# One block for the last three stages: both workspace stages and the adapter attention, with each stage's preparations placed inside the stage ahead of it

## The reference

```python
x = x + _L1_attn_a_ref(_layernorm(x, axis=-1), ...)   # gated linear attention
x = x + _L1_ffn_ref(_layernorm(x, axis=-1), ...)      # workspace stage
x = x + _L1_attn_b_ref(_layernorm(x, axis=-1), ...)   # adapter attention
x = x + _L1_ffn_ref(_layernorm(x, axis=-1), ...)      # workspace stage, same weights
```

```python
for _ in range(NB):                                   # NB = 2
    logits = _rms(x, norm_pre_w) @ compete_w.T + compete_b
    vals, idx = jax.lax.top_k(jnp.swapaxes(logits, 1, 2), k_eff)
    ...
    x_b = ctx @ out_proj_w.T + out_proj_b
    x = _rms(x + x_b, norm_post_w)
```

```python
base = jnp.einsum('bsd,od->bso', x, W)
low = jnp.einsum('bsd,brd->bsr', x, A[ids])
return base + jnp.einsum('bsr,bor->bso', low, B[ids])
```

## Time and profile before

| what | us |
|---|---|
| median of 3 executions | 2342.33 (2342.28 to 2348.39) |
| the profiled execution | 2342.52 |
| its span, first to last instruction | 2340.6 |
| workspace stage `wsa`, first product or statistic to last addition | 1705.5 to 1841.5 |
| adapter attention | 1846.1 to 2197.5 |
| workspace stage `wsb` | 2199.2 to 2333.1 |
| mean granted TensorE clock, 1 being full speed | 0.934 |

### The profile page before, as it was taken

The page is one execution under the profiler, slowest core; times in us unless marked ns, Lnnn a source line. Parts: engine busy times, 40 slices in busy tenths (PEclk is TensorE's granted clock), DMA queues, the critical chain, the costliest instruction groups (busy, mean ns, idle before and its releaser), DMA issues. The chain is left out here.

```text
span 2340.6 us, 29360 instructions
## 1 busy us (share of the span) xinstructions
PE 2006.8 (86%) x11208; PEld 1261.8 (54%) x11208; DVE 1037.4 (44%) x2255; ACT 798.4 (34%) x1757; POOL 514.9 (22%) x618
## 2 busy tenths in 40 slices
PE   7999999997499999999999998588677588889776
PEld 4556565665266766676676667222244244445443
DVE  4554545453323232333333222388644644435444
ACT  2544434352133223323332331233213234335232
POOL 2222323231111011111101000055411333342210
PEclk9999999998699999999999999689878889999788
DMA  6000000000000000000000000100000000000001
GB/s 248 1 1 1 1 1 1 1 1 31 0 1 1 1 1 1 1 1 1 1 1 1 1 1 1 65 0 1 0 1 1 1 1 1 1 1 2 1 1 37
DMA packets 9770, 23.98 MB, mean 10 GB/s; under 512 B 2448, under 2 KB 6304, under 8 KB 8864
## 3 DMA queue, kind: packets, MB, share of 16 engines
q1 hardware_dynamic: 8336, 18.92, 2.2%
q10 hardware_dynamic: 1296, 3.18, 0.4%
HBM read 20.00 MB, written 2.10 MB: 9 GB/s over the span
## 5 line engine op out<-in xcount | busy, mean ns | idle before, releaser
L1170 PEld LDWEIGHTS cos_ps<-cos_vx,cos_probs 128*128 128x128 f32 x2048 | 238.4, 191 | 33.6 <-issue 28.7
L1170 PE MATMUL cos_ps<-cos_vx,cos_probs 128*128 128x129 f32 x2048 | 239.5, 274 | 4.2 <-DVE cos_on L867 4.2
L1161 PE MATMUL cos_ps<-cos_qT,cos_kT 128*128 128x512 f32 x512 | 231.3, 596 | 1.4 <-ACT cos_qT L1023 1.4
L1052 ACT ACTIVATE cos_probs<-cos_ps 128x512 f32<-128x512 f32 x256 | 151.0, 598 | 161.9 <-PE cos_ps L1161 160.8
L366 ACT ACTIVATE probs<-sc,nmax 128x512 f32<-128x512 f32 (+3 forms) x256 | 132.6, 525 | 188.5 <-DVE nmax L229 186.4
L967 POOL TENSOR_TENSOR cos_qrs<-cos_qse,neg_half 128x4 f32<-128x4 f32 x64 | 64.5, 1008 | 511.2 <-DVE cos_qse L849 511.2
L473 PE MATMUL sc<-kT,qT 128*128 128x512 f32 (+3 forms) x512 | 171.6, 457 | 3.9 <-DVE probsT L241 2.5
L2418 DVE TENSOR_REDUCE cos_wq<-lora_ps 128x2 f32<-128x1024 f32 (+3 forms) x128 | 101.9, 824 | 104.2 <-PE lora_ps L2661 103.2
L1161 PEld LDWEIGHTS cos_ps<-cos_qT,cos_kT 128*128 128x128 f32 x512 | 94.7, 192 | 97.4 <-issue 94.1
L847 DVE TENSOR_REDUCE cos_qss<-cos_qsq 128x4 f32<-128x512 f32 x64 | 43.9, 686 | 209.1 <-ACT cos_qsq L1031 209.1
L446 PE MATMUL pq<-xnT,wap 128*128 128x512 f32 x256 | 130.1, 633 | 3.9 <-DVE swp L221 3.7
(11 more groups left out here) (466 smaller groups left out, 3449.3 us busy)
## 6 DMA issues: line engine op xcount, KB each, us to landing
onT<-in_mla_wqT SPq DMA_DIRECT2D x1, 2048.0 KB, 9.3
mla_wo<-in_mla_wo SPq DMA_DIRECT2D x1, 2048.0 KB, 19.5
cos_wq<-in_cos_wq SPq DMA_DIRECT2D x1, 2048.0 KB, 25.5
cos_wout<-in_cos_wout SPq DMA_DIRECT2D x1, 2048.0 KB, 29.9
out<-x SPq DMA_DIRECT2D x4, 512.0 KB, 2.9
x<-in_x SPq DMA_DIRECT2D x1, 1536.0 KB, 14.7
wq_pe<-in_mla_wq_pe ACTq DMA_DIRECT2D x1, 1024.0 KB, 14.3
x<-in_x SPq DMA_DIRECT2D x1, 512.0 KB, 4.2
```

Source lines behind the costliest of these rows:

```text
L1052: act.activation(probs[:, n % 2, kj, :], ps[:, kj, :], ACT.Exp).then_inc(s["e_done"], 1)
L1161: pe.matmul(ps[:, kj, :], kT[:, b % 2, kj * P:(kj + 1) * P], qT[:, hq % 2, h % 4, :], start=True, stop=True).then_inc(s["s_ready"], 1)
L1170: last = pe.matmul(po[:, qi // 2, qi % 2, :], probs[:, n % 2, kj, qi * P:(qi + 1) * P], vx[:, b % 2, kj, :], start=(kj == 0), stop=(kj == ...
```

## The change

`workspace_ffn` and `lora_attention` become `workspace_programs` and `lora_programs`: they build the queues of each engine, but open no block. A new `last_stages` opens one block and lets each engine run `first`, `lora`, `second` one after the other. There is one barrier and one clearing of semaphores at its end. One PSUM tensor serves all three. Big temporaries of the workspace stage and of the attention share one SBUF area (`room`), small ones exist once for both workspace stages (`wsp_...`), and `xf` and `xfT` lie in the memory of `cos_wq` and `cos_wout`, as `qs` and `ks` do. Where a bank or an area passes from one stage to the next, a wait on the semaphore of the last reader stands in place of the barrier (`x_before`, `free_left`).

Through hooks, parts of a stage's opening are issued inside its predecessor:

- the choice of adapters in VectorE's queue near the end of the gated linear attention;
- in the first workspace stage: the masked adapters (GpSimd, after the opening), both folds (TensorE, in `select` of rounds 0 and 1, with 20 dummy products behind them where there were 48), their additions to the weights (VectorE, in `write` between lines 1789 and 1791 of before), and behind the last `norm_sum` calls the statistics of batch 0, its normed rows and the statistics of batch 1;
- in the attention's last batch: statistics of batches 0 to 2 for the second workspace stage, their powers on GpSimd and their scaled rows on VectorE. Batch 3 stays behind the attention.

The clearing of `v` moves behind GpSimd's rotations, and the second workspace stage leaves out its constant tables, its opening dummy products and its clears of `kbd` and `vbd`. `lora_schedule`, which nothing called, is dropped.

```diff
 # gated_linear_attention, VectorE
+                dve.wait_ge(loaded, 16 * len(loads))
+                choose_adapters(dve, g)
                 gate_outputs(B - 1)
...
-def workspace_ffn(nc, g, tag, out=None):
+def workspace_programs(k, g, slots, ps, tag, early, out=None, free=None, hooks={}):
...
-        xf = sb("xf", [P, NT, D])
-        xfT = sb("xfT", [P, DC, NT * P])
-        junk = sb("junk", [P, 2, D])
+    xf = g["cos_wq"][:, :, :].rearrange("p c d -> p (c d)").rearrange("p (n d) -> p n d", d=D)
+    xfT = g["cos_wout"][:, :, :].rearrange("p h d -> p (h d)").rearrange("p (b c s) -> p b c s", b=B, c=DC)
+    junk = shared("junk", [P, 2, D])
...
     dve.tensor_tensor(wsum[:, :], bank(2)[:, 0:D], wsb[:, :], ALU.add).then_inc(s["wsum_ready"], 1)
+            hook("vector_in_write", dve, r)
     dve.wait_ge(s["wsr_ready"], r + 1)
...
+        if early == 0:
...
     dve.tensor_tensor(wsb[:, :], g["ws_start"][:, :], g["ws_write_b"][:, :], ALU.add).then_inc(s["setup"], 1)
+        if early > 0:
+            dve.drain()
+            for b in range(early, B):
+                statistics(dve, b)
+                scale_rows(dve, b)
...
                     for b in range(B):
                         norm_sum(r, b)
+                if r + 1 == WS_NB:
+                    dve.drain()
+                    hook("vector_after_batch", dve, b)
...
                 def select(r):
+            if "tensor_in_select" in hooks:
+                hook("tensor_in_select", pe, r)
+                keep_busy(20, 3)
+            else:
                     keep_busy(48, 1)
...
-LORA_OPENING = ([("rows", 0, 0), ("rows", 0, 1), ("fold", 0, "qk")] + [("qk", 0, i) for i in range(TI)]
-                + [("fold", 0, "vo"), ("v", 0, 0), ("v", 0, 1), ("turn", 0, "q"), ("turn", 0, "k"),
-                   ("rows", 1, 0), ("rows", 1, 1)])
+LORA_OPENING = ([("rows", 0, 0), ("rows", 0, 1)] + [("qk", 0, i) for i in range(TI)]
+                + [("v", 0, 0), ("v", 0, 1), ("turn", 0, "q"), ("turn", 0, "k"), ("rows", 1, 0), ("rows", 1, 1)])
+LORA_OPENING_BANKS = (0, 2, 4, 6, 1, 3, 0, 2, 4, 6, 5, 7)
+LORA_FIRST_FOLD = (1, 5)
...
+    for b in range(B):
+        for n in WS_TURN_BANKS[b]:
+            holder[n] = ("x_before", b + 1)
...
+    def add_first_fold(dve, part):
+        dve.wait_ge(s["fold_filled"], 1 + ("qk", "vo").index(part))
+        dst = wqk[:, :, :, :] if part == "qk" else wvo[:, 0, :, :, :]
+        for c in range(DC):
+            last = dve.tensor_tensor(dst[:, c, :, :], ps[:, LORA_FIRST_FOLD[c], :].rearrange("p (n d) -> p n d", n=2),
+                                     g["lora_w" + part][:, c, :, :], ALU.add)
+        last.then_inc(s["fold_ready"], 1)
...
+            if it == LAST:
+                hooks["vector_in_last"](dve)
                     for piece in lora_pieces(it):
                         empty(piece)
...
+            if LAST - LORA_GROUPS < it < LAST:
+                hooks["vector_in_batch"](dve, it - (LAST - LORA_GROUPS + 1))
...
                 zero = pool.to_reg(0.0)
-                invert(0)
-                masked_adapters(0)
                 clear_slots()
+        invert(pool, 1)
                 turn_pairs(0, 0)
-                invert(1)
                 turn_pairs(0, 3)
-                masked_adapters(1)
+        clear_values()
+        masked_adapters(pool, 1)
...
+                if u == 2 and nxt == B and r > 0:
+                    hooks["gpsimd_in_batch"](pool, r)
                         mask(it, u)
...
+def last_stages(nc, g, out):
+        def add_folds(dve, r):
+            stage["lora"]["add_first_fold"](dve, ("qk", "vo")[r])
+        def make_folds(pe, r):
+            stage["lora"]["first_fold"](pe, ("qk", "vo")[r])
+        def after_rows(dve, b):
+            if b == 0:
+                stage["lora"]["row_stats"](dve, 0)
+            elif b == 1:
+                stage["lora"]["norm_rows"](dve, 0)
+            elif b == 2:
+                stage["lora"]["row_stats"](dve, 1)
+        def adapters_for_first(pool):
+            stage["lora"]["masked_adapters"](pool, 0)
+        def after_roots(pool, b):
+            if b == 1:
+                stage["lora"]["invert"](pool, 0)
+        def rows_ahead(dve, n):
+            if n == 0:
+                stage["second"]["statistics"](dve, 0)
+                stage["second"]["statistics"](dve, 1)
+            elif n == 1:
+                stage["second"]["scale_rows"](dve, 0)
+            else:
+                stage["second"]["scale_rows"](dve, 1)
+                stage["second"]["statistics"](dve, 2)
+        def rows_in_last(dve):
+            stage["second"]["scale_rows"](dve, 2)
+        def roots_ahead(pool, r):
+            if r == 1:
+                stage["second"]["invert_variance"](pool, 0)
+                stage["second"]["invert_variance"](pool, 1)
+            elif r == 2:
+                stage["second"]["first_scales"](pool, 0)
+            else:
+                stage["second"]["first_scales"](pool, 1)
+                stage["second"]["invert_variance"](pool, 2)
+        with nc.Block() as block:
...
+            @block.tensor
+            def _(pe):
+                for name in ("first", "lora", "second"):
+                    stage[name]["by_tensor"](pe)
+        k.clear_sems()
...
-        workspace_ffn(nc, g, "wsa")
-        lora_attention(nc, g)
-        workspace_ffn(nc, g, "wsb", out)
+        last_stages(nc, g, out)
```

1657 lines of the change are left out of this document (852 added, 805 removed).

## The result

| | before | after |
|---|---|---|
| median of 4 executions, us | 2343.26 (2342.28 to 2348.39) | 2330.05 (2328.53 to 2332.58) |
| the profiled execution | 2342.52 | 2332.58 |
| its span | 2340.6 | 2330.5 |

The ratio on record, which is taken over all executions, is 0.9937 with a 95% interval of 0.9922 to 0.9953; that of the two medians is 0.9944. The changed kernel is faster by 13 us. The forecast was 2318.0 in a range of 2312 to 2326, a gain of 24.5. The sign holds, the time lies above the range, and nearly half of the expected gain is missing.

What follows compares the result with a forecast made beforehand. No engine bounds the whole; at the seams a chain through all engines sets the time. 2342.5 - 19.8 (first seam) - 11.3 (second) + 1.2 (last batch) + 5.2 (clears) + 0.2 (drains) = 2318.0 us, range 2312 to 2326.

Steps and rivals of the forecast that it cites:

- the sum: Whole kernel: 2342.5 - 19.8 - 11.3 + 1.2 + 5.2 + 0.2 = 2318.0 us, a gain of 1.0%.
- the rival of the slower clock: Attention's loop: throttle answers denser work with less clock; gain gone at mean 0.85, 2362.5 us at 0.80; chance 0.03.
- a sign of being wrong: Attention's loop, first scores to last addition: growth from 316.3 us by more than 4 would show the prediction wrong.
- First seam: First workspace stage into attention: first scores at 1861.4 instead of 1881.2, a gain of 19.8 us, bounds 17 to 22.4.
- The stall by the fill: Normed rows of batch 0 held up beside GpSimd's slot fills: between 0 and 3.4 us, taken as 1.6.
- the normed rows of batch 1: Attention's opening, just before first scores: 1.4 us plus 0.6 for the moved fill of v, ending at 1859.4.
- The rival of the low clock: Attention's opening: all four projections at half speed, about 6.8 us later, giving 2324.8; chance 0.09.
- The last batch: Attention's last batch: inserted work costs 0.3 after iteration 12, 0.7 after 13, 0.2 in 15; sum 1.2 us (0.3 to 2.8).
- Second seam: Attention into second workspace stage: bids at 2205.95 instead of 2217.26, a gain of 11.3 us, between 10 and 12.2.
- drains between the last additions: Last additions to x: the new drains between them add 0.2 us.
- The end: End of the kernel: 120 clears where 51 stood, 69 times 0.075, 5.2 us more with nothing beside them.

## Why the prediction was wrong, and where it was right

The step that failed is the sentence behind the sum, "The steady part of the attention and both rounds of both workspace stages are taken over unchanged", and beside it, in the rival of the slower clock, "Nothing in the loop's own density changes". The density did not change; the clock with which the loop starts did. From first scores to last addition the loop took 326.35 instead of 316.25, where the prediction had 1.2 more and had named 4 more as a sign of being wrong. The reading there, that the clock is lower where the loop works densest after a pause, does not fit the rows either: its first low stretch before the change, at 1888.0, lies behind 6.8 us with 6.61 of work at the high clock.

- **First seam.** Predicted 11.2 from the norms of batch 0 to the end of the normed rows; measured 11.21 (1831.56 to 1842.77). The stall by the fill was 1.55, taken as 1.6. The Trainium skill's rule on the shared ports ("SBUF — State Buffer", section "Who interferes with whom"), by which one fill costs at most its own length, agrees with the row (1.55 beside a fill of 1.89). The same rule should have been applied a second time: I charged the normed rows of batch 1 with 1.4 and the moved fill of the values with 0.6, but the fill runs beside them, and they took 2.96. The first projection came 14.07 after the norms, 0.4 sooner than worked out; with 1.0 lost at these rows and 1.7 for the projections at the low clock, the seam gave 17.5 instead of 19.8. The rival of the low clock was right in kind and far off in size: the first four of sixteen products ran low and cost 1.7, not 6.8. The sentence beside it on the rule of the Trainium skill ("TensorE: Matmul & The Clock Gate", Part 1) had 1 to 2 us, and the trace agrees with 1.7.
- **The loop's start.** 7.2 us, the largest error. Shown: filling the two pauses takes 6.1 of them away, filling one 4.1, moving the fills 7.5. Of the fourteen profiled kernels, the five that have both pauses (2.63 to 2.78 and 2.10 to 2.28: the changed kernel and those with one clearing instruction, with the rows or the second stage's preparations behind, and with dummy products at the end) all start the loop with the low stretch, and the nine others all start it at the high clock. So the cause of the stretch is the two pauses of TensorE in the last eight us ahead of the loop; in the kernel before that place had nearly unbroken work, and the long pause ended 7.6 us ahead of the scores (1873.63 to 1881.20). I had looked at the pauses only for what waits behind them. The size is less certain than the cause: with the stretch the loop start took 132.62 to 135.53, without it 126.21 to 131.91, as the low stretches further in come and go.
- **The last batch.** 0.3 and 0.7 were right (0.36 and 0.76). Behind them another 1.8 were lost where the two low stretches of 6.9 us have become one of 20.5 (from 2169.9), with 17.24 us of work in it; the experiment that takes the inserted work away gives back 2.9 in all, the one with dummy products 4.8.
- **Second seam.** 8.35 measured, 8.5 predicted. Its bids start at the low clock, and with the pauses ahead of them (3.14 and 1.27 us) filled they do not; the 1.7 us are part of the 2.2 by which the second stage is longer. The other 0.45 are three drains between the last additions, 0.15 each, where I had 0.2 for both stages.
- **The end.** 4.5 instead of 5.2, as 120 clears in a row ran at 0.071 each.
- **Chance.** The 4.2 us at the start and the 2.1 of the first workspace stage are not shown to be work of the change. Other profiled executions of kernels with the same code up to there, six in all, reach the statistics at 1704.32 to 1709.39, and take 121.9 for the stage. The kernel before took 1705.47 and 124.04 in the profile shown, and 1704.74 and 121.92 in that of the kernel with its pause filled. That the profiled execution of after stands 2.5 above its median fits this, but only one execution of it has a trace.

With the first seam, the loop's start, the last batch, the second seam and stage and the clearing corrected, the sum is 2318.0 + 2.3 + 7.2 + 1.7 + 2.0 - 0.7 - 0.2 = 2330.3, where 2330.05 was measured. Its corrections are the stages of the table without the two rows of chance, so it shows that no stage was left out, not that each term is explained; that it meets the median so closely is luck, as single executions lie 4 us apart.

What stays open is why the clock falls where TensorE has no pause. Eight of the nine kernels whose loop begins at the high clock show it five to seven us after the first scores, for seven to ten us: at 1888.0 before, at 1867.7 with the fills behind the rows, at 1881.9 with the pause filled. The ninth, with dummy products in all pauses, one clearing instruction and the fills behind the rows, keeps the high clock for the first 29 us of the loop:

```profile
1853.53:1882.50 28.97, 24.99 (x173) 12.04 (x172) 17.23 (x28) 9.90 (x15) 10.25 (x16) 1.00 0.00 1
```

The Trainium skill ("TensorE: Matmul & The Clock Gate", Part 1) knows the low clock as what idling leaves behind; the traces agree in kind for the pauses ahead of the loop, and show no idling for these stretches (6.60 busy of 6.60 in one).

## What to carry over

When a change removes waits ahead of a dense loop, look at what the tensor engine does in the last microseconds before it: two pauses of 2 to 3 us there cost about 6 us in a loop whose instructions were untouched, more than the stalls that caused them. Put fills of GpSimd behind the vector work that the chain waits for, rather than merely off the queue: beside one fill four normings took 2.95, ahead of it 1.38. And look for work that only changes its place: the clears were moved to the end at full price, while one instruction for a run of semaphores removes them (0.9937 to 0.9867). And a gain that a profile shows in one stage need not stay in the time: of the combined versions none is clearly faster than the one with that single edit.

## What the runs showed of the hardware

- A run of semaphores is cleared by one instruction: three instructions for 120 semaphores, in 0.4 us from first to last start against 8.4.
- Two pauses of 2.6 to 2.8 and 2.1 to 2.3 us within eight us were followed by 20 us at the low clock in five profiles of five; with either or both gone the loop began at the high clock.
- The granted clock fell in nearly unbroken work (6.62 busy of 6.90 before, 6.60 of 6.60 with the fills moved), and in one execution stayed low for 24 us with TensorE busy all the time, at a place where another kernel was back at the high clock after 3.5 us in the same instructions.
- The gain of a filled pause can be lost in full behind it: 2.2 us won and 2.2 us lost in the kernel before.
